# Expert tiles inside the last group iterations of a conv, attention and mixture-of-experts kernel

## The chip, the cores and the metric

The kernel runs on one core of a Trainium2 chip. The metric is the device time of one execution in microseconds (us), lower is better. The engines are TensorE (PE in the rows; PEld is its weight load), VectorE (DVE), ScalarE (ACT), GpSimd (POOL) and SyncE (SP, which only issues transfers here). Each runs its own instructions in order and waits for the others on semaphores.

## The reference

The input `x` has shape (32, 64, 16, 16). Everything is float32. Three residual blocks follow one another:

```python
x = x + conv(gn(x))        # per-channel 3x3 convolution, group norm of channel pairs
t = to_tokens(x)           # 8192 tokens of 64 channels
t = t + attn(ln(t))        # 8 heads against 32 bucket means per image, then a 64-256-64 GELU network
t = t + ffn(ln(t))         # mixture of experts
# ffn, for each token:
logits = flat @ router_w.T                  # 8 experts
gates  = the two largest softmax values, divided by their sum
h = silu(flat @ w1[e].T) * (flat @ w3[e].T) # 682 hidden units
out = sum over the two experts of gate * (h @ w2[e].T)
```

## The kernel before

**Groups.** The 32 images are worked on in 8 groups of 4 (1024 tokens). A group passes four stages: a (group norm, convolution, turn to tokens, first layer norm), b (bucket means and attention), c (second norm and GELU network), d (third norm, router, places of rows in the experts' lists). `pipeline` runs 12 iterations; in iteration i group i is in stage a, i-1 in b, i-2 in c, i-3 in d, and e=i-4 finishes on GpSimd. Each engine has its own hand-written order of the steps within an iteration, all in a function `iteration`.

**Routing.** In stage d VectorE picks two experts per token (`first_pick`, `second_pick`), TensorE counts places (`places`), VectorE turns them into row numbers (`row_places`). ScalarE copies the normed tokens into rows (`copy_rows`), and GpSimd writes them to a table in memory with 16 indirect DMAs per group (`scatter`, L497), five in the group's iteration and eleven in the next. Each expert has a region of that table.

**After the last group** TensorE counts the rows of each expert, and VectorE works out for 71 tiles of 256 rows which expert and which first row each has (`tile_expert`, `tile_row`). SyncE and ScalarE write a pad of 256 rows behind each region. SyncE then loads the weights of the tiles (four buffers) and, after all scatters have landed, their rows (eight buffers).

**A tile** t is: `turn_rows` (TensorE, two transposes), `store_xs` (ScalarE copy), three times `up(t, q)` (four matmuls of 64 rows, L757, into an h1 and an h3 bank), silu of h1 (ScalarE, L943), product with h3 (VectorE, `gated`, L1266), then `down` (six matmuls, L768), `store_results`, `turn_results`, `gate_out` (three VectorE steps, L1271 to L1277), and on GpSimd two indirect DMAs of the result rows (L519). TensorE does `up` of tile t, then `turn_rows(t+1)`, `turn_results(t-2)`, `down(t-1)`. Three h1 banks, three h3 banks and two result banks hold the tiles; all eight banks of PSUM are in use, which the group stages used before.

**The end.** When all results have landed, both result rows of a token are read back, summed with the residual and stored.

**Steps of the group stages that the text speaks of.** On GpSimd `token_rstd` (L452), `rstd2` (L458), `rstd3` (L463) raise variances to the power -1/2, `token_sum` and `unit_sum` (L468, L474) and `residual` (L481) add residuals. On VectorE `centre_scores` takes the maximum of a block of scores and subtracts it (L1096, L1098), on ScalarE `exponentials` (L848) and `store_prob` (L855) follow, on TensorE `scores` (L616), `turn_prob` (L628) and `attend` (L642). `turn_wtok` (L682) turns the third norm's tokens for the router and needs `normalise3` (L1146), which needs `rstd3`.

Of the kernel before, what the change touches and what calls it, by code (L numbers as in the profile page):

```python
# [26 lines left out]
ROW_SLOTS = 3  # L27
# [7 lines left out]
RES_SLOTS = 4  # L35
EPS = 1e-5
# [9 lines left out]
              v_heads=2 * HEADS, region=NE * NJ, scan_keep=NE * (NJ + 1), k_rows=T // MT, tile_no=1, tile_at=1,  # L46
              pad=2 * ROW, q_one=1, k_one=1)
SMALLS = dict(bias2=1, g1=1, b1=1, g2=1, b2=1, fc1_bias0=2, proj=C + M + 2 * C, fc1=DFF, fc2=2 * C, fc2_bias=C,
              router=NE)
# [14 lines left out]
def hybrid_block(nc, x, consts, smalls, weights, out):  # L64
    with ExitStack() as ctx:
# [31 lines left out]
        k_rows = const_of("k_rows")  # L97
        tile_no = const_of("tile_no")
# [64 lines left out]
        ssub = sb("ssub", [P, 2, 2 * HEADS, M])  # L163
        prob = sb("prob", [P, 2, 4, P])
# [44 lines left out]
        tile_expert = sb("tile_expert", [P, 1], U32)  # L209
        tile_row = sb("tile_row", [P, 1], U32)  # L210
# [28 lines left out]
        k_ps = bk34[0:C + 1, 0, 0:P]  # L239
        v_ps = bk34[:, 1, 0:256].rearrange("p (b c) -> p b c", b=GB)  # L240
        fc1_ps = [bk7, bk6]
        y_ps = bk7.rearrange("p (j c) -> p j c", j=NJ)
        l_ps = bk67[:, :, 0:NJ // 2 * NE].rearrange("p a (q e) -> p a q e", e=NE)
        pos_ps = bk7[:, 64:64 + NE * NJ].rearrange("p (e j) -> p e j", e=NE)
# [3 lines left out]
        xt_ps = h1_ps[0][:, 0:MT]  # L248
        yt_banks = [bk0, bk7]
# [77 lines left out]
        pos_counted = sem("pos_counted")  # L327
        sums_kept = sem("sums_kept")
# [3 lines left out]
        counted = sem("counted")  # L332
# [31 lines left out]
        def _(sp):  # L364
# [8 lines left out]
            for a in range(2, NG):  # L373
                sp.wait_ge(xn_ready, 2 * (a - 1))
                sp.wait_ge(xres_ready, 2 * (a - 1))
                load_x(a)

            sp.wait_ge(pads_ready, 1)
            write_pad(sp, NE * REG)
            for e in range(NE // 2):  # L380
                write_pad(sp, sp.value_load(pad_row[0:1, e:e + 1], min_val=0, max_val=NE * REG - MT))

            def load_weights(t):
                wait(sp, down_done, t - W_SLOTS + 1)
                expert = sp.value_load(tile_expert[t:t + 1, 0:1], min_val=0, max_val=NE - 1)
# [3 lines left out]
            def load_rows(t):  # L389
                wait(sp, y_scattered[t % X_SLOTS], 32 * (t // X_SLOTS))  # L390
                row = sp.value_load(tile_row[t:t + 1, 0:1], min_val=0, max_val=NE * REG)
# [3 lines left out]
            sp.wait_ge(sched_ready, 1)  # L395
            for t in range(W_SLOTS - 1):
                load_weights(t)
            sp.wait_ge(pads_written, 16 * (NE + 1))
            for b in range(ROW_SLOTS):
                sp.wait_ge(scattered[b], 2 * NJ * 16 * ((NG - b + ROW_SLOTS - 1) // ROW_SLOTS))  # L400
            for t in range(X_SLOTS - 2):
                load_rows(t)
            for t in range(W_SLOTS - 1, NT):
                load_weights(t)
                if t + X_SLOTS - 1 - W_SLOTS < NT:
                    load_rows(t + X_SLOTS - 1 - W_SLOTS)
# [10 lines left out]
        def _(pool):  # L417
# [8 lines left out]
            g.memset(picked[:, :, 0:1], 0.0)  # L426
            pool.wait_ge(consts_loaded, 16)
# [73 lines left out]
            def iteration(a=None, b=None, c=None, d=None, e=None):  # L501
                run(a, group_rstd)
                run(c, residual)
                run(c, rstd2)
                run(e, scatter, 5, 11)
                run(a, token_rstd)
                run(d, row_destinations)
                run(d, scatter, 0, 5)
                run(c, rstd3)
                run(a, token_sum)  # L510
                run(a, unit_sum)

            pipeline(iteration)

            for t in range(NT):
                pool.wait_ge(yout_ready, t + 1)
                pool.sem_inc(waited, 1)
                for h in range(2):
# [4 lines left out]
                        .then_inc(y_scattered[t % X_SLOTS], 16)  # L523

        @block.tensor
        def _(pe):
# [49 lines left out]
            def queries(b):  # L576
                wait(pe, probt_ready, 4 * b)
                for h in range(2):
                    last = mm(bk34[0:C + 1, h, :], q_aug[:, :], n1t[:, h * 512:(h + 1) * 512], start=True, stop=True)
                last.then_inc(q_ready, 1)  # L580
# [15 lines left out]
            def keys(b):  # L596
                pe.wait_ge(pooledt_ready, b + 1)
                pe.wait_ge(qt_ready, b + 1)
                mm(k_ps, k_aug[:, :], pooled_t[:, :], start=True, stop=True).then_inc(k_ready, 1)

            def values(b):
                pe.wait_ge(rep_ready, b + 1)
                pe.wait_ge(qt_ready, b + 1)
                for m in range(GB):
                    last = mm(bk34[:, 1, m * C:(m + 2) * C].rearrange("p (r c) -> p r c", r=2),
# [4 lines left out]
            def scores(b, p):  # L610
                if p == 0:
                    pe.wait_ge(kblk_ready, b + 1)
                wait(pe, ssub_ready, 4 * b + p - 1)
                for bp in range(2):
                    j, m = 2 * p + bp, 2 * (p // 2) + bp
                    last = mm(bk12[:, p % 2, bp * 256:(bp + 1) * 256], qt[:, j * P:(j + 1) * P],  # L616
                              kblk[:, m, :, :].rearrange("c h m -> c (h m)"), start=True, stop=True)
                last.then_inc(s_ready, 1)

            def turn_prob(b, p):  # L620
                pe.wait_ge(prob_ready, 4 * b + p + 1)
                if p == 0:
                    pe.wait_ge(kblk_ready, b + 1)
                if p == 1:
                    pe.wait_ge(vblk_ready, b + 1)
                wait(pe, probt_ready, 4 * b + p - 1)
                for a in range(4):
                    last = turn(bk34[:, p % 2, a * P:(a + 1) * P], prob[:, p % 2, a, :], ident)  # L628
                last.then_inc(probt_turned, 1)

            def attend(b, p):
                pe.wait_ge(probt_ready, 4 * b + p + 1)
                if p == 0:
                    pe.wait_ge(vblk_ready, b + 1)
                    wait(pe, att_read, 2 * b)
                if p == 2:
# [11 lines left out]
            def turn_n2(c):  # L648
                pe.wait_ge(n2_ready, c + 1)
                wait(pe, lsub_ready, c)  # L650
                for q in range(NJ // 2):
                    last = turn(bk6[:, q * P:(q + 1) * P], n2[:, 2 * q:2 * q + 2, :].rearrange("p a c -> p (a c)"), ident)
                last.then_inc(n2_turned, 1)

            def fc1(c, a):
                if a == 0:
                    pe.wait_ge(n2t_ready, c + 1)
                    wait(pe, pos_ready, c)
                for par in range(2):
                    if a == 1:  # L660
                        pe.wait_ge(hid_ready, 4 * c + par + 1)
                    at = slice(par * C, (par + 1) * C)
                    mm(fc1_ps[par], fc1_s[at, a * P:(a + 1) * P], n2t[at, :], start=True, stop=True)\
                        .then_inc(fc1_ready, 1)

            def fc2(c):
                pe.wait_ge(hid_ready, 4 * c + 4)
                for q in range(NJ // 2):
                    for par in range(2):
                        j = 2 * q + par  # L670
                        n = min(2, NJ - j)
                        for a in range(2):
                            last = mm(y_ps[:, j:j + n, :], hid[:, a, par, q * P:(q + 1) * P],  # L673
# [4 lines left out]
            def turn_wtok(c):  # L678
                pe.wait_ge(wtok_ready, c + 1)
                pe.wait_ge(hid_ready, 4 * c + 4)  # L680
                for q in range(NJ // 2):
                    last = turn(bk6[:, q * P:(q + 1) * P], wtok[:, 2 * q:2 * q + 2, :].rearrange("p a c -> p (a c)"), ident)  # L682
                last.then_inc(wt_turned, 1)

            def router(d):
                pe.wait_ge(wt_ready, d + 1)
                pe.wait_ge(t2_ready, d + 1)
                for q in range(NJ // 2):
                    for par in range(2):
                        at = slice(par * C, (par + 1) * C)  # L690
# [712 lines left out]
```

## Time and profile before

| | us |
|---|---|
| runs shown | 805.01, 802.60, 799.39 (median 802.6) |
| the profiled execution | 802.19 |
| its span, first to last instruction | 800.4 |
| TensorE busy | 650.6 (81%) |
| VectorE, ScalarE, GpSimd busy | 463.2, 353.7, 371.8 |

Busy time is a sum over stages that have different limits; a busy TensorE is not one at its peak, and its granted clock, 0.851 in the mean, has the two levels 0.5 (1.2 GHz) and 1 (2.4 GHz). What bounds a stage is read from that stage.

### The profile page before, as it was taken

The numbers are of one execution on the slowest core, as the hardware profiler recorded it, in microseconds if no ns is written. First come the engines' busy times: TensorE is split into PE (matmuls) and PEld (weight loads), VectorE is DVE, ScalarE is ACT, GpSimd is POOL, SyncE is SP. The second block draws the span as 40 slices with busy tenths as digits, with TensorE's granted clock in tenths as the row PEclk, the third lists the DMA queues.
The fourth block names the chain that finished last, engine by engine and source line by source line (L and its number), as shares of the span: only waits on it lengthen the run. The fifth ranks groups of instructions, "written<-read, shape, count | busy, mean of one in ns | idle before, by whom it ended". The sixth has DMA issues, their size and how long they took to land.

```text
span 800.4 us, 13968 instructions
## 1 busy us (share of the span) xinstructions
PE 650.6 (81%) x4632; PEld 487.2 (61%) x4632; DVE 463.2 (58%) x1094; ACT 353.7 (44%) x693; POOL 371.8 (46%) x377
## 2 busy tenths in 40 slices
PE   2597989797979797866206999999999999999960
PEld 2475858585857576664104777677777777777740
DVE  2356677686868676643502566655555665555545
ACT  1143646373727273533203555455555445555520
POOL 2204241767676768727670343334444333444440
PEclk9667868797978788575656999999999999999995
DMA  2000000010101010101173455555556455554608
GB/s 85 0 14 1 14 1 14 19 49 17 51 18 38 18 38 17 51 5 53 50 182 86 148 161 160 165 161 162 179 161 167 152 168 168 179 156 150 191 8 314
DMA packets 46615, 75.47 MB, mean 94 GB/s; under 512 B 7488, under 2 KB 30048, under 8 KB 46544
## 3 DMA queue, kind: packets, MB, share of 16 engines
q1 hardware_dynamic: 34512, 57.12, 24.5%
q0 software_dynamic: 8640, 12.74, 4.8%
q10 hardware_dynamic: 3392, 4.73, 1.8%
q8 instruction: 37, 0.61, 0.3%
q14 instruction: 34, 0.28, 0.1%
HBM read 58.54 MB, written 16.47 MB: 94 GB/s over the span
## 4 chain that ended last, share of the span: by engine, by line
PE 49%; POOL 23%; issue 17%; DVE 6%; DMA 3%; ACT 1%; POOLq 0%; SPq 0%; ACTq 0%; DVEq 0%
PE bk L757 25%; POOL expert_rows L497 15%; PE bk L768 12%; PE bk L745 3%; POOL rr L452 3%; PE bk L775 2%; POOL r L463 1%; PE bk L554 1%; POOL r L458 1%; POOL x2t L481 1%; DMA out<-hid 1%; DMA srow<-expert_results 1%; PE bk L642 1%; POOL grstd L441 1%; PE bk L616 1%
## 5 line engine op out<-in xcount | busy, mean ns | idle before, releaser
L1266 DVE TENSOR_TENSOR units<-bk,silu 128x512 f32<-128x512 f32 x213 | 147.3, 692 | 165.7 <-ACT silu L943 165.7
L519 POOL DMA_INDIRECT expert_results<-yout,xin x142 | 139.5, 983 | 218.3 <-DVE yout L1277 191.5
L757 PE MATMUL bk<-xs,wbuf 64*128 64x256 f32 x1704 | 205.5, 388 | 1.1 <-ACT xs L930 1.1
L757 PEld LDWEIGHTS bk<-xs,wbuf 64*128 64x128 f32 x1704 | 160.8, 189 | 44.4 <-issue 26.6
L943 ACT ACTIVATE silu<-bk 128x512 f32<-128x512 f32 x213 | 127.2, 597 | 87.2 <-PE bk L757 87.2
L497 POOL DMA_INDIRECT expert_rows<-srow,pos x128 | 132.4, 1034 | 44.2 <-issue 37.9
L768 PE MATMUL bk<-units,wbuf 128*64 128x256 f32 x852 | 107.6, 388 | 0.0
L768 PEld LDWEIGHTS bk<-units,wbuf 128*64 128x64 f32 x852 | 54.8, 136 | 32.4 <-issue 11.7
L935 ACT ACTIVATE ysb<-bk 128x256 f32<-128x256 f32 x71 | 27.2, 383 | 84.3 <-PE bk L768 84.3
L452 POOL TENSOR_TENSOR rr<-vare,c_mhalf 128x16 f32<-128x16 f32 x8 | 23.4, 2923 | 74.6 <-DVE vare L1046 74.6
L745 PE MATMUL bk<-const,xin 128*128 128x128 f32 x142 | 31.3, 302 | 29.2 <-DMA xin<-expert_rows 29.2
L745 PEld LDWEIGHTS bk<-const,xin 128*128 128x128 f32 x142 | 14.3, 141 | 52.5 <-issue 52.5
L930 ACT ACTIVATE xs<-bk 128x256 f32<-128x256 f32 x71 | 26.8, 378 | 34.7 <-PE bk L745 34.7
L642 PEld LDWEIGHTS bk<-vblk,prob_t 128*128 128x128 f32 x256 | 35.4, 205 | 6.9 <-ACT prob_t L855 5.0
L642 PE MATMUL bk<-vblk,prob_t 128*128 128x144 f32 x256 | 38.5, 308 | 0.2 <-ACT prob_t L855 0.2
L616 PE MATMUL bk<-kblk,qt 65*128 65x256 f32 x128 | 37.8, 435 | 0.0
L554 PE MATMUL bk<-const,hsum 128*128 128x128 f32 x192 | 35.0, 333 | 0.0
L848 ACT ACTIVATE prob<-ssub 128x512 f32<-128x512 f32 x32 | 19.4, 626 | 34.1 <-DVE ssub L1098 34.0
L1096 DVE TENSOR_REDUCE smax<-bk 128x16 f32<-128x512 f32 x32 | 21.8, 681 | 21.3 <-PE bk L616 21.2
L673 PEld LDWEIGHTS bk<-small,hid 128*128 128x128 f32 x256 | 31.2, 200 | 2.4 <-ACT hid L871 2.4
L616 PEld LDWEIGHTS bk<-kblk,qt 65*128 65x128 f32 x128 | 26.7, 226 | 9.2 <-DVE ssub L1098 5.3
L554 PEld LDWEIGHTS bk<-const,hsum 128*128 128x128 f32 x192 | 32.1, 246 | 0.0
(184 smaller groups left out, 963.2 us busy)
## 6 DMA issues: line engine op xcount, KB each, us to landing
wbuf<-in_weights SPq DMA_DIRECT2D x71, 576.0 KB, 4.1
xin<-expert_rows SPq DMA_DIRECT2D x71, 130.0 KB, 2.4
expert_results<-yout,xin POOLq DMA_INDIRECT x142, 2.8
xg<-in_x SPq DMA_DIRECT2D x8, 256.0 KB, 2.8
expert_rows<-srow,pos POOLq DMA_INDIRECT x128, 2.4
srow<-expert_results SPq DMA_DIRECT2D x8, 256.0 KB, 5.1
srow<-expert_results ACTq DMA_DIRECT2D x8, 256.0 KB, 5.9
out<-hid ACTq DMA_DIRECT2D x8, 256.0 KB, 5.2
```

The lines of the kernel that those rows point to most:

```text
L452: g.tensor_tensor(rr[:, :, :].rearrange("p a j -> p (a j)"), vare1[:, :, :].rearrange("p a j -> p (a j)"), c_mhalf[:, :], ALU.pow).then_in ...
L497: g.indirect_dma_start(rows[0:NE * REG, :], bass.IndirectOffsetOnAxis(ap=pos[:, d, k, j:j + 1], axis=0), srow[:, d % ROW_SLOTS, k, j, :], ...
L519: g.indirect_dma_start(results[:, :], bass.IndirectOffsetOnAxis(ap=xin[:, t % X_SLOTS, h, ROW - 1:ROW].bitcast(U32), axis=0), yout[:, t % ...
L554: last = mm(o, hsum[:, s, h0 + dy:h0 + dy + 8, :], ident, start=False, stop=dy == 2)
L616: last = mm(bk12[:, p % 2, bp * 256:(bp + 1) * 256], qt[:, j * P:(j + 1) * P], kblk[:, m, :, :].rearrange("c h m -> c (h m)"), start=True, ...
L642: last = mm(bk5[:, at:at + 2 * (C + HEADS)].rearrange("p (r c) -> p r c", r=2), prob_t[:, p % 2, 2 * bp + ch, :], vblk[:, m, ch, :].unsque ...
L673: last = mm(y_ps[:, j:j + n, :], hid[:, a, par, q * P:(q + 1) * P], fc2_s[:, a, :].unsqueeze(1).broadcast_to([P, n, C]), start=a == 0, sto ...
L745: last = turn(xt_ps[:, h * P:(h + 1) * P], xin[:, t % X_SLOTS, h, 0:2 * C], ident)
L757: last = mm(bank[:, ch * MT:(ch + 1) * MT], wbuf[part, t % W_SLOTS, at:at + P], xs[part, t % 2, :], start=True, stop=True)
L768: last = mm(yt_banks[t % 2][ch * C:(ch + 1) * C, 0:MT], wbuf[:, t % W_SLOTS, at:at + C], units[:, t % 2, q, ch * MT:(ch + 1) * MT], start= ...
L943: f(silu[:, q, :], h1_ps[q], ACT.Silu).then_inc(silu_ready, 1)
L1266: tt(units[:, t % 2, q, :], h3_ps[q], silu[:, q, :], ALU.mult).then_inc(unit_ready, 1)
```

## The change

The pipeline stays as it is for iterations 0 to 4 (`ramp`). From iteration 5 (`MIX`) to 10 the iterations are mixed (`mix`): in each, 16 slots between group steps hold beats, and a beat is a third of an expert tile, one `up(t, q)` with what hangs on it. `slot_beats` gives 27 beats (nine tiles) to iteration 5, none in its slots 0 to 4, and 24 (eight tiles) to the others: one in each of slots 0 to 7, two in each of slots 8 to 15. The score and attention steps stand between slots 9 and 10 with no beats. The 49 mixed tiles are followed by a tail of 22 in the old order.

The tiles of a round come from `schedule(d)`, which runs on VectorE behind each group from d = 1 and picks tiles whose 256 rows are full by then; the last round, for the tail, takes the rest. A round's first `load_rows` waits for the scatters of all groups up to its own. All 16 scatters of a group now run in the group's own iteration, in iterations 5 to 10 four by four behind `token_rstd` and between slots 10 to 13.

PSUM is divided anew in the mixed part: three banks are a ring for h1 and h3 (two per beat), one bank (`bk7`) holds the turned rows and the results of a tile, one bank (`shared`) in turn holds scores, n2, y and wtok, one (`turned`) queries, values and turned probabilities. Probabilities before the turn get four buffers where they had two; row buffers go from three to two. The router multiplies both halves of its input at once. The expert counts come from `places` of each group. All nine pads are written by SyncE.

```diff
+MIX = 5
+FIRST_ROUND = 1
+ROUND_TILES = [0, 9, 8, 8, 8, 8, 8]
+MIXED = sum(ROUND_TILES)
+SLOTS_A, SLOTS_S = 10, 6
-ROW_SLOTS = 3
+ROW_SLOTS = 2
+def slot_beats(i):
+    if i == MIX:
+        return [0, 0, 0, 0, 0, 2, 2, 2, 2, 2, 3, 3, 3, 3, 3, 2]
+    return [1, 1, 1, 1, 1, 1, 1, 1, 2, 2, 2, 2, 2, 2, 2, 2]
...
+        ring = [bk12[:, 1, :], bk34[:, 1, :], bk6]
+        def ring_banks(k):
+            return ring[2 * k % 3], ring[(2 * k + 1) % 3]
...
@@ SyncE
             def load_rows(t):
+                r = ROUND_OF[t]
+                s = t - ROUND_AT[r]
+                if s == 0:
+                    for b in range(ROW_SLOTS):
+                        sp.wait_ge(scattered[b], 2 * NJ * 16 * ((r - b) // ROW_SLOTS + 1))
...
+            def beat(t, q):
+                if q == 0:
+                    load_tile(t + W_SLOTS - 1)
@@ GpSimd
+            def beat(t, q):
+                if q == 2 and t > 0:
+                    scatter_results(t - 1)
+            def mixed_iteration(i, a=None, b=None, c=None, d=None):
+                run(c, residual)
+                beats(i, 0, beat)
+                beats(i, 1, beat)
+                run(c, rstd2)
+                run(d, rstd3)
+                beats(i, 2, beat)
+                run(a, group_rstd)
+                for k in range(3, SLOTS_A):
+                    beats(i, k, beat)
+                run(d, row_destinations)
+                run(a, token_rstd)
+                run(d, scatter, 0, 4)
+                beats(i, 10, beat)
+                run(d, scatter, 4, 4)
+                beats(i, 11, beat)
+                run(d, scatter, 8, 4)
+                run(a, token_sum)
+                run(a, unit_sum)
+                beats(i, 12, beat)
+                run(d, scatter, 12, 4)
+                beats(i, 13, beat)
...
@@ TensorE
+            def ring_free(k):
+                for earlier, first in ((k - 2, False), (k - 1, True)):
...
+                        elif first:
+                            pe.wait_ge(silu_ready, NU * x + y + 1)
+                        else:
+                            pe.wait_ge(unit_ready, NU * x + y + 1)
...
+            def turn_rows(t):
+                pe.wait_ge(xin_loaded[t % X_SLOTS], 16 * (t // X_SLOTS + 1))
+                if t < MIXED:
+                    wait(pe, yout_ready, t - 2)
...
+            def beat(t, q):
...
+                up(t, q)
+                if q == 0 and t + 1 < MIXED:
+                    turn_rows(t + 1)
+                if q == 1 and t > 0:
+                    down(t - 1)
+                if q == 2 and t > 0:
+                    turn_results(t - 1)
...
+                beats(i, 9, beat)
+                run(b, scores, 0)
+                run(a, convolution, 0)
+                run(b, scores, 1)
+                run(a, convolution, 1)
+                run(b, scores, 2)
+                run(d, places)
+                run(b, scores, 3)
+                run(b, turn_prob, 0)
+                run(b, turn_prob, 1)
+                run(c, fc1, 0)
+                run(b, attend, 0)
+                run(b, attend, 1)
+                run(b, turn_prob, 2)
+                run(c, fc1, 1)
+                run(b, turn_prob, 3)
+                run(b, attend, 2)
+                run(b, attend, 3)
+                beats(i, 10, beat)
+                run(c, fc2)
...
@@ ScalarE, slots 0, 1 and 7 to 10
+                run(b, store_n1t, 1)
+                beats(i, 0, beat)
+                run(c, squares2)
+                run(d, squares3)
+                beats(i, 1, beat)
...
+                run(a, add_x)
+                run(b, key_blocks)
+                beats(i, 7, beat)
+                run(d, copy_rows)
+                run(c, store_n2t)
+                beats(i, 8, beat)
+                beats(i, 9, beat)
+                run(d, router_exp)
+                run(b, exponentials, 0)
+                run(b, exponentials, 1)
+                run(a, store_tokens)
+                run(b, exponentials, 2)
+                run(b, exponentials, 3)
+                run(b, store_prob, 0)
+                run(b, store_prob, 1)
+                run(a, squares1)
+                run(c, gelus, 0)
...
@@ VectorE, score part
+                run(b, centre_scores, 0)
+                run(d, first_pick)
+                run(b, centre_scores, 1)
+                run(d, second_pick)
+                run(b, centre_scores, 2)
+                run(a, centre1)
+                run(d, row_places)
+                run(b, centre_scores, 3)
+                run(a, variance1)
+                run(b, attended, 0)
+                run(d, schedule)
+                run(a, normalise1)
+                run(b, attended, 1)
+                beats(i, 10, beat)
```

## Rows read from the trace of the kernel before

**Rows 1.** windows: us, busy of PE, PEld, DVE, ACT, POOL, then PEclk, DMA share, GB/s
```profile
182.04:222.99 40.95, 34.85 (x226) 27.75 (x224) 30.74 (x80) 22.02 (x43) 29.63 (x28) 0.83 0.10 33
401.00:427.40 26.40, 0.66 (x2) 0.29 (x2) 0.00 (x0) 0.40 (x2) 14.68 (x16) 0.50 0.62 146
433.60:761.40 327.80, 327.80 (x2718) 233.22 (x2718) 193.51 (x406) 166.12 (x339) 129.70 (x132) 1.00 0.54 162
```

**Rows 2.** timeline of GpSimd in iterations 4 and 5; start, duration, engine, line, output and input
```profile
176.13 2.93 POOL L452 TENSOR_TENSOR rr<-vare,c_mhalf 128x16 f32<-128x16 f32 x1 [3.15 <-DVE vare L1046]
...
187.02 2.13 POOL L463 TENSOR_TENSOR r<-vare,c_mhalf 128x8 f32<-128x8 f32 x1
189.13 1.27 POOL L468 TENSOR_TENSOR u_tok<-tok,small 128x512 f32<-128x512 f32 x1
190.48 1.59 POOL L474 TENSOR_TENSOR u_tok<-u_tok,u 128x512 f32<-128x512 f32 x1
...
196.20 1.26 POOL L481 TENSOR_TENSOR x2t<-u_tok,att 128x512 f32<-128x512 f32 x1
197.42 1.67 POOL L458 TENSOR_TENSOR r<-vare,c_mhalf 128x8 f32<-128x8 f32 x1
```

**Rows 3.** timeline of TensorE at the start of iteration 5; idle time before in brackets
```profile
182.04 2.21 PE L642 MATMUL bk<-vblk,prob_t 128*128 128x144 f32 x16
...
192.35 0.59 PE L544 MATMUL bk<-chvar,const 128*128 128x2 f32 x2 [4.41 <-DVE chvar L1016]
192.80 1.09 PE L682 MATMUL bk<-const,wtok 128*128 128x128 f32 x4
```

**Rows 4.** timeline of all engines over one expert tile
```profile
520.21 2.86 PE L757 MATMUL bk<-xs,wbuf 64*128 64x256 f32 x24
...
521.38 0.60 ACT L943 ACTIVATE silu<-bk 128x512 f32<-128x512 f32 x1 [0.66 <-PE bk L757]
...
522.00 0.69 DVE L1266 TENSOR_TENSOR units<-bk,silu 128x512 f32<-128x512 f32 x1 [1.56 <-ACT silu L943]
...
523.59 1.52 PE L768 MATMUL bk<-units,wbuf 128*64 128x256 f32 x12
...
524.34 0.28 DVE L1271 COPY ysum<-bk 128x128 f32<-128x128 f32 x1
...
524.98 0.29 DVE L1277 TENSOR_TENSOR yout<-ysum,xin 128x128 f32<-128x128 f32 x1
...
525.03 2.86 PE L757 MATMUL bk<-xs,wbuf 64*128 64x256 f32 x24
```

**Rows 5.** timeline from the last scatters to the first tile
```profile
419.57 0.96 POOL L497 DMA_INDIRECT expert_rows<-srow,pos  x1 [0.30 <-issue]
420.83 0.96 POOL L497 DMA_INDIRECT expert_rows<-srow,pos  x1 [0.30 <-issue]
...
426.28 0.66 PE L745 MATMUL bk<-const,xin 128*128 128x128 f32 x2 [29.21 <-DMA xin<-expert_rows]
```

**Rows 6.** timeline of VectorE in the routing and score steps
```profile
201.90 0.22 DVE L1161 SCALAR_TENSOR_TENSOR peq<-lsub,const 128x64 f32<-128x64 f32 x1
...
207.74 0.69 DVE L1096 TENSOR_REDUCE smax<-bk 128x16 f32<-128x512 f32 x1 [0.96 <-PE bk L616]
...
214.35 0.69 DVE L1098 TENSOR_TENSOR ssub<-bk,smax 128x512 f32<-128x512 f32 x1
```

**Rows 7.** groups by line and shape: count, busy us, mean ns, idle before and its releaser
```profile
L519 POOL DMA_INDIRECT expert_results<-yout,xin x142 | 139.5, 983 | 218.3 <-DVE yout L1277 191.5 <-issue 26.8
...
L848 ACT ACTIVATE prob<-ssub 128x512 f32<-128x512 f32 x32 | 19.4, 626 | 34.1 <-DVE ssub L1098 34.0
...
L848 ACT ACT_TABLE_LOAD x7 | 9.0, 1283 | 0.1
...
L886 ACT ACTIVATE srow<-wtok 128x1024 f32<-128x1024 f32 x16 | 16.1, 1064 | 0.0
```

**Rows 8.** windows, one stretch of iteration 6; columns as in rows 1
```profile
231.00:241.20 10.20, 7.91 (x43) 4.40 (x43) 6.02 (x19) 2.60 (x4) 7.16 (x9) 0.50 0.01 2
```

More of the change, by code:

```diff
@@ L499, in scatter, with scatter_results @@
                         srow[:, d % ROW_SLOTS, k, j, :], None).then_inc(scattered[d % ROW_SLOTS], 16)
[L501 to L515, printed above, removed]
+            def scatter_results(t):
                 pool.wait_ge(yout_ready, t + 1)
@@ L574, in rotate, with queries @@
                 last.then_inc(rot_ready, 1)
[L576 to L580, printed above, removed]
+            def queries(b, h):
+                if h == 0:
+                    wait(pe, probt_ready, 4 * b)
+                elif mixed(b + 1):
+                    pe.wait_ge(qt_ready, 2 * b + 1)
+                mm(q_bank(b, h)[0:C + 1, :], q_aug[:, :], n1t[:, h * 512:(h + 1) * 512], start=True, stop=True)\
+                    .then_inc(q_ready, 1)
             def bucket_sums(b):
@@ L697, in places @@
                 pe.wait_ge(passed_ready, d + 1)
-                mm(pos_ps, before, picked[:, :, 1:NJ + 1], start=True, stop=False)
-                mm(pos_ps, ones, passed[:, :, 0:NJ], start=False, stop=True).then_inc(pos_counted, 1)
-            def iteration(a=None, b=None, c=None, d=None, e=None):
+                if mixed(d + 3):
+                    if d + 2 < NG:
+                        pe.wait_ge(kblk_ready, d + 3)
+                    pe.wait_ge(att_read, 2 * min(d + 2, NG))
+                bank = place_bank(d)
@@ L732, in iteration @@
                 run(a, turn_n1, 0)
-            pipeline(iteration)
-            pe.wait_ge(sums_kept, NG)
-            pe.wait_ge(pos_ready, NG)
-            mm(bk7[:, 0:NE], ones, picked[:, :, 0], start=True, stop=True).then_inc(counted, 1)
-            pe.wait_ge(sched_ready, 1)
-            def turn_rows(t):
-                pe.wait_ge(xin_loaded[t % X_SLOTS], 16 * (t // X_SLOTS + 1))
-                wait(pe, silu_ready, NU * (t - 1) + 1)
-                for h in range(2):
-                    last = turn(xt_ps[:, h * P:(h + 1) * P], xin[:, t % X_SLOTS, h, 0:2 * C], ident)
-                last.then_inc(xt_turned, 1)
@@ L780, in _ @@
+            ramp(iteration)
+            mix(mixed_iteration)
+            turn_rows(MIXED)
+            for t in range(MIXED, NT):
                 for q in range(NU):
@@ L1205, in iteration, with beat @@
+            def beat(t, q):
+                gated(t, q)
+                if q == 2 and t > 0:
+                    gate_out(t - 1)
+            def iteration(i, a=None, b=None, c=None, d=None, e=None):
                 run(a, channel_statistics)
```

674 lines of the change are left out of this document (467 added, 207 removed).

## The prediction, made before the result

> **What bounds the kernel now.** I read the windows by stage first, then the timelines of GpSimd and TensorE, then the groups. The run has four parts: eight group iterations, their drain, a gap, and 71 expert tiles. A full group iteration takes 40.95 us and TensorE is busy for 34.85 of it, part of that at the lower clock; the gap costs 26.4 us with TensorE all but idle; in the tiles TensorE is busy 327.80 of 327.80 us at full clock [rows 1]. So the tiles are bound by TensorE, and nothing in them waits. A group iteration is bound by GpSimd's queue: sixteen scatters, 1.26 us from one to the next [rows 5], are 20.2 us, and with the power instructions and sums [rows 2] the queue has some 35 us of work in 41.
>
> The change wants to put tiles into TensorE's idle time. There is less of it than the page suggests. At full clock the group steps of an iteration are about 31 us of TensorE (34.85 less half of the 7.91 that it is busy in a stretch like the one at 1.2 GHz [rows 1, 8]); eight tiles are 8 x 4.82 = 38.6 (520.21 to 525.03, [rows 4]); together 69.5 against 40.95 + 38.6 = 79.5 now. Only if the mixed iteration comes under 79.5 does it gain.
>
> **Up to the first tile.** TensorE starts iteration 5 at 182.0 [rows 3], in both kernels. In the new GpSimd order iteration 4 issues all sixteen scatters of group 1 behind the token power (176.13 to 179.06): 0.85 wait for the iota and 16 x 1.265 end them at 200.2; two sums (1.27, 1.59) at 203.1; then residual 1.26, second and third power 1.67 and 2.13 [rows 2]: 208.2. normalise3 and the transposes of wtok stand behind that; now they start at 192.8 [rows 3], then at about 210. Rows turned and copied, the first `up` starts at 213. That is 31 us of iteration 5 for group steps that took about 20.
>
> **A tile in the mixed part** has one result bank and three ring banks, so each `up` waits for the silu of the beat before it. The prices are read from [rows 4]: the silu ends 1.77 after its `up` starts (521.38 + 0.60 - 520.21), the product 0.71 later, gate_out's three steps 0.93 later still (524.34 to 525.27). turn_rows of the next tile waits for that gate_out: 3.46 after the last `up` of the tile before. Then turn 0.3, `up` 0.93, `down` 1.45, and the next last `up` starts at 6.15. So a bare mixed tile takes 6.15 where it now takes 4.82; group steps of TensorE can fill the difference only in the slots that have any.
>
> **A full mixed iteration (6 and 7)**, followed along its queues:
> - Slots 0 to 9 (four tiles and the first group half): TensorE's work is 19.3 + about 11. Where it stands still: 1.4 for the squares, which wait on ScalarE ahead of a silu until VectorE has done channel statistics and two centrings; 2.5 in pair_variances, whose VectorE step is behind two variances; 2.3 for a silu behind key_blocks, copy_rows (2 x 1.06, [rows 7]) and n2t; 3 in several short ones. Sum 39.4.
> - The score part, one score bank and no tiles. VectorE's order is gate_out of the last tile (ends 2.25 after TensorE starts the part), four centre_scores, first_pick, second_pick, centre1, row_places. Now the same steps run from 201.90 to 215.04 with one centre_scores fewer (1.40), normalise2 (0.6), vblk (0.7) and a wait (0.96) more [rows 6]: 12.3 to 12.8. Then exp 0.63 [rows 7], prob copy, turn, copy, squares (0.6 each) and a reduction with two small steps, 0.9: the variance for token_rstd is ready 19.4 after the start. TensorE is through at 25.
> - GpSimd from there: power 2.93, 16 scatters 20.2, results of two tiles 4 x 1.285 = 5.1 (0.98 each plus issue, [rows 7]), two sums 2.9, and 3.7 waiting, since the results of tile 3 are gated out only 36 after the part's start while GpSimd reaches them earlier. Sum 34.8.
> - The next round's first tile may hold rows of this group: SyncE holds its row load until all sixteen scatters landed, and TensorE turns those rows right behind `up(7,0)`, in order. From the end of the last scatter to the turn it is 4.5 now (421.79 to 426.28, [rows 5]). TensorE gets to this turn 23 after the score part's end by bare tiles, some 11 before the rows are there. Behind it stand turn 0.3, two `up`, `down` and a turn: 3.9.
> 39.4 + 19.4 + 34.8 + 4.5 + 3.9 = 102.
>
> ScalarE switches tables up to three times in such an iteration (exp, gelu, silu), where the group steps alone need two. A load takes 1.28 and no idle time stands behind it: the idle time before the exponentials is all VectorE's [rows 7]. Two of the three loads lie under VectorE's list, the gelu's is in the 25 above. The Trainium skill (ScalarE: Activation LUTs, What ACT_TABLE_LOAD costs) adds a drain of about 1.4 to each load; by that the sum would be some 7 us higher. The row decides against it.
>
> The new `schedule`, 17 small VectorE steps, is about 4.3 by the row of the smallest steps (0.2 each and more, [rows 6]); it has attended's wait beside it in iterations 5 to 8 and costs nothing there, and about 4 in iterations 9 and 10, where the next products are queued behind it. SyncE's loads of the other seven tiles are issued two tiles ahead: nothing, or a row load of about 2 if SyncE is late. SyncE writes the pads, all nine now, with the load for the tail's first tile, three tiles ahead: the same late scatters hide them.
>
> **The others.** Iteration 5 has nine tiles in slots 5 to 15: 23 for slots 5 to 9, 25 for scores, 5.7 x 6.15 + 3.6 (fc2) less 0.6 for the rest, 2.6 at the row wait: 89, ending at 302. Iteration 8 has no a-stage: 34 to the scores, row_places at 12.4, then scatters, results (waiting until tile 3's at 34.9) and row load to 58.5: 93. Iteration 9 has c and d only: 32 + 46 = 78. Iteration 10: 28 + 38.6 = 66.5 to the first tail rows.
>
> **The tail.** From the first turned rows to the end of the span is now 374.1 us for 71 tiles [rows 5]; less 49 x 4.82 = 236.2 it is 138 for 22. The profiled run lies 1.8 over its span.
>
> **Sum:** 182 + 31 + 89 + 102 + 102 + 93 + 78 + 66.5 + 138 + 1.8 = 883. The clock: TensorE stood still for 4.41 us before 192.35 [rows 3] and likewise one iteration later, and from 231.0 to 241.2 it was granted 0.50, the lower level of 1.2 GHz [rows 8]. The waits of 4 in the score part and 11 at the rows should bring such stretches too. That costs nothing where VectorE or GpSimd ends last, and up to 4 + 3 in an iteration where the tiles do: 0 to 33 over six. I take 7, as the late scatters cover most of it. **Forecast 890**, against 802.19 of the profiled run, which is within 0.1% of the median of 802.6, so it is taken for that too.
>
> **Rivals.**
> 1. *GpSimd keeps up*: the scatters go out fast enough that rows never hold TensorE. For: its queue has some 53 us of work in 100. Against: the order puts all scatters behind token_rstd. Then iterations end by TensorE's own chain (39.4 + 25 + 28 = 92.4; 85, 70, 62 for the last): 182 + 120 + 185 + 217 + 138 + 2 = 844; were slots 0 to 9 free of stalls too (7.4 less in iterations 6 and 7, some 6 in 5 and 8), 817. Chance 0.20.
> 2. *The clock* is at its lower level wherever waits break up the beats, and the products and scatters follow: 883 + 33 = 916. For: [rows 8]. Against: TensorE has more work between waits than now. The Trainium skill (TensorE: Matmul & The Clock Gate, Loop structure matters more than you think) holds that matmuls parted by waits run cold and the loop nest decides it; by that rule this rival holds, and [rows 3, 8] agree for a wait of 4.4. Chance 0.20.
> 3. *Faster*: TensorE is the bound, tiles and group steps fill each other. Iterations then take 69.5, and 65, 47, 41 for the last three. With iteration 5 ending at 280 (210, nine tiles 43, the other group steps some 25): 280 + 139 + 153 + 138 + 2 = 712 at the very best, 797 with half of the 171 us between it and the sum; so it is faster if more than half of my waits are not there, or the six iterations average under 80 from 182 on ((802 - 1.8 - 138 - 182) / 6). I put it at 770. For: VectorE has only 30.74 + 8 x 3 = 55 of work in such an iteration [rows 1, 4]. Against: the score part alone holds VectorE for 15 us before the fourth ssub. Chance 0.08; another 0.04 that gains and losses cancel.
> 4. The forecast's case: 0.48.
>
> **Range and chances.** 815 to 930: from the first rival's low end to the second's 916 with a row load late in each iteration (6 x 2). Within 1% is what runs of this kernel can't tell from none (799.4 to 805.0). Faster 0.08, same 0.04, slower 0.88.
>
> **What would show it.** GpSimd's line of scatters directly behind rr, ending late in slot 12 or after; TensorE idle some 10 us per iteration before a turn of xin, released by the DMA of expert_rows; a wait of about 4 in each score part before turn_prob; first `up` near 213; the tail beginning near 745. I am wrong if mixed iterations come in at 80 or less, if the wait for rows is missing (then near 845), or if TensorE's clock is low for most of the mixed part.

## The result, and the profile after

The changed kernel takes 929.7 us (median of 4; 927.3 to 934.6) against 801.2 of the kernel before beside it: 1.161 times as long, 95% interval 1.158 to 1.164. The forecast was 890, range 815 to 930, "slower" at 0.88. The direction came out and most of the waits did; the size did not, by 40 us: the time lies at the upper end of the range. The profiled execution took 934.56, its span is 932.5, and all times below are from it.

The page of the changed kernel: span, TensorE's row of busy time, the granted clock in 40 slices, and the shares of the chain that ended last.
```profile
span 932.5 us, 14259 instructions
PE 709.0 (76%) x4582; PEld 487.2 (52%) x4582; DVE 476.2 (51%) x1206; ACT 365.8 (39%) x708; POOL 366.7 (39%) x378
PEclk9576977968899888977989778888978979899995
PE 44%; DVE 17%; issue 13%; POOL 12%; ACT 7%; DMA 5%; SPq 0%; POOLq 0%; ACTq 0%; DVEq 0%
```
The clock row is the first thing to see: four slices in a row at 9 come only in the tail. VectorE, behind which no tile of the kernel before waited, has 17% of the chain, and TensorE is idle for 24% of the span that was to be filled.

The timeline of TensorE at the six turns of rows that had to wait for the row load (in brackets the wait):
```profile
303.32 0.44 PE L866 MATMUL bk<-const,xin 128*128 128x128 f32 x2 [3.88 <-DMA xin<-expert_rows]
412.77 0.69 PE L866 MATMUL bk<-const,xin 128*128 128x128 f32 x2 [10.07 <-DMA xin<-expert_rows]
523.34 0.69 PE L866 MATMUL bk<-const,xin 128*128 128x128 f32 x2 [11.32 <-DMA xin<-expert_rows]
628.78 0.69 PE L866 MATMUL bk<-const,xin 128*128 128x128 f32 x2 [8.39 <-DMA xin<-expert_rows]
717.64 0.69 PE L866 MATMUL bk<-const,xin 128*128 128x128 f32 x2 [7.83 <-DMA xin<-expert_rows]
793.24 0.69 PE L866 MATMUL bk<-const,xin 128*128 128x128 f32 x2 [5.28 <-DMA xin<-expert_rows]
```
These turns mark out the iterations, so the sum can be laid against them. The prediction's terms for iterations 5 to 7 end 3.9 behind a turn, so their turns were at 302 - 3.9 = 298.1 and so on; those for 8 to 10 end at the turn itself (in iteration 8 the 58.5 runs up to the row load):

| turn of rows that ends | predicted at | measured at | interval predicted | measured |
|---|---|---|---|---|
| iteration 5 | 298.1 | 303.32 | | |
| iteration 6 | 400.1 | 412.77 | 102 | 109.45 |
| iteration 7 | 502.1 | 523.34 | 102 | 110.57 |
| iteration 8 | 599 | 628.78 | 96.9 | 105.44 |
| iteration 9 | 677 | 717.64 | 78 | 88.86 |
| iteration 10 (tail's first rows) | 743.5 | 793.24 | 66.5 | 75.60 |
| end of the span | 881.5 | 932.5 | 138 | 139.3 |

Every mixed iteration is longer than predicted; the first turn (+5.2) and the tail (+1.3) are nearly right.

Windows over iteration 6 of the changed kernel, columns as in [rows 1]:
```profile
309.20:321.10 11.90, 8.43 (x64) 5.88 (x62) 10.10 (x19) 4.45 (x9) 3.24 (x3) 0.99 0.43 128
321.10:334.80 13.70, 12.69 (x56) 6.08 (x56) 7.41 (x24) 3.18 (x7) 7.38 (x8) 0.51 0.02 5
334.80:353.00 18.20, 15.34 (x115) 10.19 (x114) 8.49 (x20) 12.42 (x31) 4.00 (x4) 1.00 0.29 88
365.50:372.30 6.80, 3.96 (x13) 2.16 (x13) 2.40 (x7) 3.92 (x6) 0.64 (x1) 0.51 0.00 0
402.70:412.80 10.10, 0.03 (x2) 0.03 (x1) 0.98 (x2) 0.60 (x1) 6.38 (x7) 0.67 0.18 52
412.80:418.70 5.90, 5.90 (x33) 3.44 (x34) 0.69 (x1) 1.55 (x4) 0.00 (x0) 0.69 0.38 121
```
The second row is the one the prediction priced too low: for 13.7 us TensorE is granted the lower level, 1.2 GHz, while it is busy for 12.69 of them (7.91 of 10.20 in [rows 8]). The work itself runs at half speed and, as experiment 2 shows, sets the end. What went before it is short: waits of 2.29 and 1.21 us, at 319.39 and 322.11. The last two rows are the wait for the rows and the 5.9 us behind it, where turn, two `up`, `down` and a turn were put at 3.9.

### The profile page after: what moved, and what is told of

Same layout as the page of the kernel before. It is cut to its first block, busy times and chain, and to the rows that moved or that the text cites. A ratio compares the mean times of both kernels' runs of the same rounds, so it can differ in the third digit from the quotient of the medians.

```text
span 932.5 us, 14259 instructions
## 1 busy us (share of the span) xinstructions
PE 709.0 (76%) x4582; PEld 487.2 (52%) x4582; DVE 476.2 (51%) x1206; ACT 365.8 (39%) x708; POOL 366.7 (39%) x378
## 4 chain that ended last, share of the span: by engine, by line
PE 44%; DVE 17%; issue 13%; POOL 12%; ACT 7%; DMA 5%; SPq 0%; POOLq 0%; ACTq 0%; DVEq 0%
PE bk L883 17%; PE bk L899 9%; POOL expert_rows L576 7%; ACT silu L1142 3%; PE bk L773 2%; DVE units L1543 2%; PE bk L821 2%; PE bk L809 2%; PE bk L866 2%; POOL expert_results L584 2%; PE bk L696 2%; DMA expert_rows<-srow,pos 2%; DMA xin<-expert_rows 1%; DMA srow<-expert_results 1%; DVE ssub L1388 1%
## 5 line engine op out<-in xcount | busy, mean ns | idle before, releaser
L883 PE MATMUL bk<-xs,wbuf 64*128 64x256 f32 x1704 | 251.5, 425 | 37.0 <-ACT silu L1142 33.7
L883 PEld LDWEIGHTS bk<-xs,wbuf 64*128 64x128 f32 x1704 | 166.8, 202 | 103.4 <-issue 72.0
L576 POOL DMA_INDIRECT expert_rows<-srow,pos x128 | 127.5, 996 | 55.4 <-issue 38.8
L899 PE MATMUL bk<-units,wbuf 128*64 128x256 f32 x852 | 119.6, 421 | 0.0
L899 PEld LDWEIGHTS bk<-units,wbuf 128*64 128x64 f32 x852 | 59.5, 148 | 48.5 <-issue 30.7
L773 PE MATMUL bk<-vblk,prob_t 128*128 128x144 f32 x256 | 40.6, 315 | 1.1 <-ACT prob_t L1089 1.1
L757 PE MATMUL bk<-const,prob 128*128 128x128 f32 x128 | 22.5, 308 | 16.1 <-ACT prob_t L1089 12.4
L669 PE MATMUL bk<-const,hsum 128*128 128x128 f32 x192 | 33.0, 319 | 0.0
L739 PEld LDWEIGHTS bk<-kblk,qt 65*128 65x128 f32 x128 | 23.8, 204 | 15.8 <-DVE ssub L1388 12.7
L906 PE MATMUL bk<-const,ysb 128*128 128x128 f32 x142 | 30.6, 298 | 1.0 <-ACT ysb L1136 1.0
```

The lines of the kernel that those rows point to most:

```text
L576: g.indirect_dma_start(rows[0:NE * REG, :], bass.IndirectOffsetOnAxis(ap=pos[:, d, k, j:j + 1], axis=0), srow[:, d % ROW_SLOTS, k, j, :], ...
L669: last = mm(o, hsum[:, s, h0 + dy:h0 + dy + 8, :], ident, start=False, stop=dy == 2)
L739: last = mm(score_bank(b, p)[:, bp * 256:(bp + 1) * 256], qt[:, j * P:(j + 1) * P], kblk[:, m, :, :].rearrange("c h m -> c (h m)"), start= ...
L773: last = mm(bk5[:, at:at + 2 * (C + HEADS)].rearrange("p (r c) -> p r c", r=2), prob_t[:, p % 2, 2 * bp + ch, :], vblk[:, m, ch, :].unsque ...
L883: last = mm(bank[:, ch * MT:(ch + 1) * MT], wbuf[part, t % W_SLOTS, at:at + P], xs[part, t % 2, :], start=True, stop=True)
L899: last = mm(y_bank(t)[ch * C:(ch + 1) * C, 0:MT], wbuf[:, t % W_SLOTS, at:at + C], units[:, t % 2, q, ch * MT:(ch + 1) * MT], start=q == 0 ...
```

## Experiments

Kernels are the changed one with the edits named; ratios are to the kernel before, on the same chip. Fill matmuls are matmuls whose results nothing reads.

**1. Scatters early.** If rows hold TensorE because twelve scatters stand behind token_rstd and the sums, issuing them right behind the first four must remove the wait.
```
-                run(d, scatter, 4, 4)
+                run(d, scatter, 4, 12)
...
-                run(d, scatter, 8, 4)
...
-                run(d, scatter, 12, 4)
```


> One change to the new kernel: on GpSimd the twelve scatters that stood behind slots 10, 11 and 12 follow the first four at once. Theory R (TensorE waits for rows because GpSimd issues a group's last scatters late): in iteration 6 the power ends at 374.6, 16 x 1.27 later is 394.9, the rows are turned 4.5 later at 399.4, and TensorE asks for them at 402.7. The waits of 3.9, 10.1, 11.3, 8.4, 7.8 and 5.3 us before the turns of xin are gone, 47 us, and the half clock behind them, some 2 each: 870 to 885. Rival (another wait takes its place, the tiles' results now late or the next group step): 915 or more.

Measured 880.0 us, ratio 1.097 (1.093 to 1.101): 50 us back. GpSimd's timeline in iteration 6, first of the changed kernel, then of this one:
```profile
371.66 2.94 POOL L531 TENSOR_TENSOR rr<-vare,c_mhalf 128x16 f32<-128x16 f32 x1 [13.30 <-DVE vare L1336]
...
390.78 1.00 POOL L584 DMA_INDIRECT expert_results<-yout,xin  x1 [5.29 <-DVE yout L1554]
...
407.36 0.96 POOL L576 DMA_INDIRECT expert_rows<-srow,pos  x1 [0.31 <-issue]
```
```profile
365.74 2.93 POOL L531 TENSOR_TENSOR rr<-vare,c_mhalf 128x16 f32<-128x16 f32 x1 [13.31 <-DVE vare L1334]
...
388.61 0.96 POOL L576 DMA_INDIRECT expert_rows<-srow,pos  x1 [0.30 <-issue]
389.87 1.00 POOL L584 DMA_INDIRECT expert_results<-yout,xin  x1 [0.31 <-issue]
```
From the power to the last scatter's start it is 35.7 in the changed kernel and 22.9 here. In between stood 5.29 of waiting for a result, four result scatters and two sums; results and sums now come behind, and nothing waits. Of the row waits only the tail's is left (5.03 at 740.13), which was expected to go too. The low clock in the slots stays: slots 0 to 9 of iteration 6 still take 43.7 (303.43 to 347.15), so the row waits are not what brings it. Iteration 6 shrinks by 11.6, from 109.5 (309.18 to 418.69) to 97.9 (303.43 to 401.31): the wait of 10.07, and most of the 2.0 of low clock behind it.

**2. Fill matmuls in the short waits.** If the clock costs the rest, feeding TensorE in the waits of slots 0 to 9 and of the score part must give time back though it adds work.
```
                 run(b, rotate)
+                if b is not None:
+                    pe.wait_ge(t2_ready, i - 2)
+                    fill(5, shared)
                 beats(i, 2, beat)
+                if a is not None:
+                    fill(3, shared)
                 run(a, pair_variances)
...
                 run(b, turn_prob, 0)
+                if a is not None:
+                    pe.wait_ge(tok_ready, a + 1)
+                if b is not None:
+                    fill(8 if a is not None else 4)
...
```
In iterations 8 to 10 there are some more of them between the scores and ahead of places.

> One change to the new kernel: TensorE fills its other waits with matmuls whose results nobody reads (ident by the constants, 128x256), 5 after rotate and 3 before pair_variances in slots 1 and 2, and 8 between turn_prob 0 and 1; in iteration 8 also 5 and 4 in place of the convolution and 4 between turn_prob 0 and 1, in 9 and 10 twelve before places. It costs TensorE time only where a wait stood. Theory C (the 40 us that my sum lacks are the lower clock behind short waits): the stretches at 0.5 in slots 2 to 5 and in the score part shrink, iterations 6 to 8 are 6 to 10 us shorter, 9 and 10 some 4: 890 to 910. Rival (the clock is not the cause, the sum lacks other waits): 925 to 940, the fills cost what they take.

Measured 905.4 us, ratio 1.129 (1.125 to 1.133): 24 us back. Windows over slots 0 to 9 of iteration 6 and over the rest up to the turn, in the changed kernel and in this one:
```profile
309.20:353.10 43.90, 36.57 (x234) 22.25 (x233) 26.00 (x61) 20.14 (x46) 14.62 (x15) 0.84 0.24 73
353.10:412.80 59.70, 40.87 (x277) 29.26 (x275) 28.81 (x83) 21.48 (x36) 29.87 (x28) 0.89 0.19 60
```
```profile
303.50:341.60 38.10, 34.15 (x250) 22.64 (x249) 25.82 (x61) 20.02 (x46) 14.39 (x15) 1.00 0.28 84
341.60:400.80 59.20, 44.06 (x293) 32.72 (x291) 28.86 (x83) 21.41 (x36) 29.80 (x28) 0.91 0.19 61
```
The slots take 38.1 at clock 1.00 with 16 instructions more, 43.9 at 0.84 without them: 5.8 us of clock. The prediction's 39.4, made for full clock, holds. The score part and the scatters behind it take 59.2 and 59.7, where 58.7 was predicted (19.4 + 34.8 + 4.5): there VectorE and GpSimd end last and TensorE's clock buys nothing.

Iteration 7 did not gain like this. The stretch at the lower level went from the middle of the slots and came back at their end, behind a wait of 1.62 at 440.38; the first of the slow `up`s, which takes 1.13 at full clock:
```profile
442.54 2.08 PE L883 MATMUL bk<-xs,wbuf 64*128 64x256 f32 x8
```
The slots take 41.1 there (408.06 to 449.12), and from the turn of rows before (400.76) to its own (511.05) iteration 7 is 0.3 shorter than in the changed kernel, where 6 to 10 were expected. Iteration 6 is 6.0 shorter, 8 is 8.3, 9 is 3.0 and 10 is 1.9 (their turns at 297.28, 608.21, 694.07 and 767.82).

**3. Both.**

> Both edits of the two kernels before. If R and C hold and don't overlap, the gains add up: 840 to 860. If the rows and the clock are one cause (the long wait brings all of the low clock), the result is that of the early scatters alone, 870 to 885.

Measured 858.7 us, ratio 1.072 (1.068 to 1.077): 71 us back, 50 and 24 nearly added. Its windows over the same stretches:
```profile
303.60:341.70 38.10, 34.16 (x250) 22.63 (x249) 25.82 (x61) 20.02 (x46) 14.39 (x15) 1.00 0.27 84
341.70:395.60 53.90, 48.26 (x324) 35.28 (x323) 29.54 (x84) 22.97 (x40) 29.74 (x28) 0.97 0.25 79
```
An iteration is 92.0 (303.61 to 395.61), the first rival's 92.4. So without the row waits and most of the low clock the change still loses 57 us: 92 is over the 79.5 that eight tiles and an iteration take apart.

**4. Order at the start.** Iteration 4 keeps the third power ahead of the eleven scatters, which would let wtok (the third norm's tokens, turned for the router), and with it the first tile, go earlier if that power held the start up.
```
-                if last:
-                    run(d, scatter, 5, 11)
-                else:
-                    run(c, rstd3)
+                run(c, rstd3)
...
+                if i == MIX:
+                    run(d - 1, scatter, 5, 11)
```


> On the new kernel: iteration 4 keeps the old order on GpSimd (five scatters, then the third power), and the other eleven scatters of group 1 follow in iteration 5 behind the three powers. If my reading of the start is right (sixteen scatters and four other steps in a row, the first tile can't start before group 1 has landed): the transposes of wtok come 18 us earlier, near 193, but the first tile's rows are turned at 214 to 218, no earlier than now (212.5), and the total is the same within 5 us. Rival (the late third power alone holds the first tile): the first up comes 10 us or more earlier and the total falls by as much.

One execution, 937.2 us. TensorE's timeline, of the changed kernel and of this one:
```profile
211.62 1.11 PE L833 MATMUL bk<-const,wtok 128*128 128x128 f32 x4 [8.59 <-DVE wtok L1436]
...
214.67 1.65 PE L883 MATMUL bk<-xs,wbuf 64*128 64x256 f32 x6 [1.50 <-ACT xs L1131]
```
```profile
198.25 1.12 PE L833 MATMUL bk<-const,wtok 128*128 128x128 f32 x4
...
219.49 0.66 PE L866 MATMUL bk<-const,xin 128*128 128x128 f32 x2 [20.12 <-DMA xin<-expert_rows]
```
The turn of wtok comes 13 earlier, and the first rows, now behind later scatters, come at 219.5 instead of 212.5, later than the 214 to 218 expected. What it gives it takes: the first tile is bound by group 1's scatters whichever goes first. The total is 2.6 over the profiled execution of the changed kernel; a single run shows no more than that nothing was won.

**5. Tiles in iterations 9 and 10 alone.** With MIX = 9 no iteration that holds all of a, b, c and d is mixed; scatters early. If a mixed drain fills time that TensorE idles anyway, this beats the kernel before.
```
-MIX = 5
-FIRST_ROUND = 1
-ROUND_TILES = [0, 9, 8, 8, 8, 8, 8]
+MIX = 9
+FIRST_ROUND = MIX - 4
+ROUND_TILES = [0] * FIRST_ROUND + [9] + [8] * (10 - MIX)
```


> Mixed iterations start at 9 in place of 5 (17 mixed tiles, 54 in the tail), with the early scatters. Where the old pipeline drains, TensorE has little group work and the old kernel stood still for 26 us before its first tile. Theory M (mixing loses where a group iteration is full, since each queue's order and the score part then hold the tiles, and gains only in the drain): iterations 9 and 10 take some 90 and 65 for 17 tiles: 780 to 800, at or a little under the kernel before. Rival (tiles mixed in lose anywhere, by their own 6.2 us and the late scatters): 815 or more.

Measured 806.6 us, ratio 1.006 (1.004 to 1.008). A miss: 73 us better than experiment 1, which has the same scatters, but not faster. Part of what is lost stands in the bare tiles, whose turns of rows are 6.3 apart:
```profile
428.24 0.41 PE L864 MATMUL bk<-const,xin 128*128 128x128 f32 x2 [0.44 <-DVE yout L1552]
...
432.99 1.14 PE L881 MATMUL bk<-xs,wbuf 64*128 64x256 f32 x8 [0.40 <-ACT silu L1140]
434.56 0.41 PE L864 MATMUL bk<-const,xin 128*128 128x128 f32 x2 [0.44 <-DVE yout L1552]
```

**6. The same with a fourth ring bank.** In iterations 9 and 10 the banks of steps a and b are free: one joins the ring, and turned rows go into the convolution's. The waits for a free bank are loosened to match.
```
-        ring = [bk12[:, 1, :], bk34[:, 1, :], bk6]
+        ring = [bk12[:, 1, :], bk34[:, 1, :], bk6, turned]
...
-            return bk7[:, MT:2 * MT] if t < MIXED else h1_ps[0][:, 0:MT]
+            return bk0[:, 0:MT] if t < MIXED else h1_ps[0][:, 0:MT]
```


> The kernel that mixes from iteration 9 with early scatters (806.6), with one thing more: in those two iterations no image is in the first two stages, so the bank of queries and turned probabilities joins the ring (four banks) and the turned rows go to the bank of the convolution. A beat then waits for the one two before it, not for the last silu, and turn_rows not for gate_out. Theory T (a mixed tile costs 6.15 to 6.3 us in place of 4.82 because of three ring banks and one result bank): 17 tiles x 1.3 = 22 us less: 780 to 792. Rival (the mixed tiles are held by the other queues, not by banks): 800 to 808.

Measured 792.4 us, ratio 0.987 (0.984 to 0.990): 1.3% faster than the kernel before. The same turns:
```profile
407.54 0.44 PE L859 MATMUL bk<-const,xin 128*128 128x128 f32 x2
...
412.91 0.44 PE L859 MATMUL bk<-const,xin 128*128 128x128 f32 x2
...
418.29 0.44 PE L859 MATMUL bk<-const,xin 128*128 128x128 f32 x2
```
5.4 apart and without a wait. Over 17 mixed tiles 0.95 each are 16 us; 14 came back, where 22 were expected. Most of what a bare mixed tile takes over 4.82 [rows 4] is the sharing of banks.

**7. Iteration 10 alone.** As 6, but MIX = 10 and nine tiles.

> The same with mixing in iteration 10 alone: nine mixed tiles, 62 in the tail. They run while the last group is routed and scattered, where the kernel before had TensorE idle for 26 us (401 to 427). Theory M (mixing pays where the pipeline drains): 780 to 792, about that of mixing from 9, since iteration 9 has still a full c-stage. Rival (iteration 9's own waits are the larger gain): 795 to 805.

Measured 799.7 us, ratio 0.997 (0.996 to 0.999), the rival's number. TensorE's waits show where it went:
```profile
399.13 1.11 PE L828 MATMUL bk<-const,wtok 128*128 128x128 f32 x4 [18.21 <-DVE wtok L1427]
...
428.01 0.69 PE L849 MATMUL bk<-picked,const 128*128 128x64 f32 x2 [5.17 <-DVE passed L1464]
...
467.75 0.69 PE L859 MATMUL bk<-const,xin 128*128 128x128 f32 x2 [5.87 <-DMA xin<-expert_rows]
```
Wherever mixing begins, the iteration ahead of it puts the scatters before the third power, and wtok pays once: 18.2 here, 12.0 in experiment 6. One mixed iteration covers little more than that.

**8. Scores first.** On experiment 3: the four centre_scores ahead of the routing picks on VectorE, places behind fc1.
```
                 run(b, centre_scores, 0)
-                run(d, first_pick)
                 run(b, centre_scores, 1)
-                run(d, second_pick)
                 run(b, centre_scores, 2)
                 run(a, centre1)
-                run(d, row_places)
                 run(b, centre_scores, 3)
+                run(d, first_pick)
+                run(d, second_pick)
                 run(a, variance1)
+                run(d, row_places)
```


> On the new kernel with early scatters and warm fills (858.7): VectorE does the four centre_scores first and first_pick, second_pick and row_places behind them, TensorE's places stands behind fc1. Theory S (the score part is held by VectorE's list, in which the routing steps stand between the scores): the fourth ssub comes 3 to 4 us earlier in iterations 5 to 8, the turned probabilities with it, and the parts shorten by 2 to 4 each: 845 to 853. Rival (one score bank holds it, each scores waits for the ssub before, whatever stands between): 856 to 862.

Measured 857.2 us, ratio 1.070 (1.065 to 1.075), against 858.7: nothing, as the rival had it. Yet the score part did get shorter, from 24.95 (341.68 to 366.63) to 23.4 (337.83 to 361.25). Windows over the last beats ahead of it and over most of it, of experiment 3 and of this one:
```profile
337.40:341.70 4.30, 4.21 (x33) 2.65 (x34) 1.38 (x2) 1.80 (x5) 1.94 (x2) 1.00 0.05 17
341.70:366.60 24.90, 22.25 (x128) 17.88 (x126) 17.59 (x60) 12.58 (x19) 7.07 (x6) 0.93 0.11 36
```
```profile
332.00:338.00 6.00, 5.82 (x33) 3.52 (x34) 1.42 (x3) 2.04 (x5) 1.95 (x2) 0.72 0.04 12
338.00:361.00 23.00, 19.91 (x125) 16.32 (x125) 17.61 (x58) 12.27 (x19) 8.05 (x7) 1.00 0.13 41
```
A short stretch at the lower level lay inside the score part; it now lies ahead of it, in 33 instructions that take 5.8 instead of 4.2. From the last waiting turn to the first `up` behind the part it is 29.1 in both (337.49 to 366.63, 332.18 to 361.25). Why the stretch moved, no run shows.

**9. Fill matmuls in the fastest version.** On experiment 6, in its four waits: 40 ahead of the first turn of wtok, 16 ahead of each places, 26 ahead of the tail's rows.

> The kernel with tiles in iterations 9 and 10 alone, four ring banks and early scatters (792.4 us), with fill matmuls whose results nothing reads where TensorE waits: 40 before the first turn of wtok (12.0 us of waiting), 16 before each places (5.2 and 5.4), 26 before the turned rows of the tail (8.0). Theory C (a wait leaves TensorE at 1.2 GHz for a while after it, and that is lost where TensorE ends last): behind each of the four waits about 8 to 10 us of work run at half clock in that kernel, 3 to 4 us lost each; with the fills 780 to 787. Rival (the late part is bound by the rows' arrival and by the waits' own ends, so the clock after them changes little): 790 to 794.

Measured 792.0 us, ratio 0.986 (0.984 to 0.988): the same as without, the rival's case. TensorE's timeline at the tail's first rows, of experiment 6 and of this one:
```profile
492.23 0.69 PE L859 MATMUL bk<-const,xin 128*128 128x128 f32 x2 [8.02 <-DMA xin<-expert_rows]
...
498.02 0.44 PE L859 MATMUL bk<-const,xin 128*128 128x128 f32 x2
```
```profile
490.07 11.39 PE L843 MATMUL bk<-const 128*128 128x256 f32 x52
501.30 0.38 PE L864 MATMUL bk<-const,xin 128*128 128x128 f32 x2
504.94 0.44 PE L864 MATMUL bk<-const,xin 128*128 128x128 f32 x2
```
The next turn follows 3.6 behind the rows instead of 5.8, so the fills do their work. But each takes 0.44, and 26 of them take 11.4 where the wait was 8.0; the first 40 end 5.2 after wtok is there (366.14 + 0.69, and the turn at 372.00). What the clock gives back, the surplus of fills takes: they were too many, and fewer were not tried.

## Why the prediction was right in direction and wrong in size

**Right.** TensorE is not free to fill: the iteration's chain runs through VectorE's score list and GpSimd's scatters, and in iteration 6 with fills it is 38.1 + 59.2 against a predicted 39.4 + 58.7. The row wait was named at "some 11" and is 10.07 and 11.32, and early scatters remove it. The tail for 22 tiles was 138, measured 139.3. The score part's power starts 18.6 after the part (353.06 to 371.66), predicted 19.4, and from there to the end of the last scatter (408.32) it is 36.7, predicted 34.8: that their sum fits so well is partly luck. The bare mixed tile was worked out at 6.15; from the last `up` of one to that of the next it is 6.33 in the changed kernel:
```profile
393.34 1.14 PE L883 MATMUL bk<-xs,wbuf 64*128 64x256 f32 x8
...
396.82 0.41 PE L866 MATMUL bk<-const,xin 128*128 128x128 f32 x2 [0.44 <-DVE yout L1554]
...
399.67 1.13 PE L883 MATMUL bk<-xs,wbuf 64*128 64x256 f32 x8
```
The wait on yout, the one result bank, stands where it was put.

Table loads cost no more than their row. In the changed kernel (groups of ScalarE: busy, mean ns, idle before):
```profile
L1105 ACT ACT_TABLE_LOAD x8 | 10.3, 1283 | 0.1
L1142 ACT ACT_TABLE_LOAD x7 | 9.0, 1283 | 0.1
L1126 ACT ACT_TABLE_LOAD x6 | 7.7, 1283 | 0.1
```
There are 25 of them in all, at 1283 ns, and nothing like a drain stands ahead of them. The Trainium skill (ScalarE: Activation LUTs, What ACT_TABLE_LOAD costs) has the same 1283 and a drain beside it; these rows show the first and not the second.

**Wrong: the clock term.** The step that failed is "I take 7, as the late scatters cover most of it". The runs show some 30 in the slots and behind the row waits alone. Slots 0 to 9 are not covered by the scatters of their own iteration, which are issued later; there TensorE ends last, and each of iterations 6 to 8 loses some 6: 43.9 against 38.1 with fills; 43.8 in iteration 7 (418.69 to 462.44) against 38.1 in experiment 3 (395.61 to 433.69); 41.0 (530.24 to 571.25) against 35.0 with fills (517.82 to 552.82) in iteration 8. That is about 17.5. Behind the row waits the beats run at the lower level too, here in iteration 8, where an `up` takes 1.13 and `down` 1.52 at full clock:
```profile
629.40 2.08 PE L883 MATMUL bk<-xs,wbuf 64*128 64x256 f32 x8
631.41 2.83 PE L899 MATMUL bk<-units,wbuf 128*64 128x256 f32 x12
```
From the turn of rows to the turn of results it is 5.6, 5.7, 6.6, 6.8 and 6.8 behind the five waits, and 3.95 in experiment 3 (391.39 to 395.34): some 12 more. So the term is about 30, an estimate from these rows. Experiment 2 fills no row wait; of the 24 that it gave back, 3.0 and 1.9 lie in iterations 9 and 10, which the 30 leaves out. With them the clock comes to some 34, at the prediction's upper bound of 33 or past it; that bound is itself less than six times the 4 + 3 that it names. The Trainium skill (TensorE: Matmul & The Clock Gate, Loop structure matters more than you think) says that the loop nest decides whether matmuls stay warm and that a long DMA wait between them makes them cold; the `up` of 2.08 behind the row wait agrees. Here waits of only 1.2 to 2.3 us between beats, none of them for a DMA, also went ahead of such a stretch. The second rival, at 0.20 and 916, was the nearest to the result, and its mechanism came out in the slots and behind the row waits.

**What else the sum lacked.** Of the 51.6 between 883, the sum ahead of the clock term, and the profiled 934.56, the clock is some 34. The terms for iterations 8 and 9 leave out the 3.9 behind the row wait, which 5, 6 and 7 have: 7.8. The first row wait ended 5.2 late, of which 1.7 were there at the first `up` (214.67 for 213) and 2.9 went with the fills of experiment 2, so are clock too (from the first scores of iteration 5 to the turn, 238.80 to 303.32 and 235.62 to 297.28). The other 4 or so are smaller differences, such as iteration 7 from the scores on (60.9 against 58.7), and were not run down one by one.

**The third rival (faster)** fell on its price. With row waits and most of the low clock removed an iteration is still 92.0 and not 69.5. Of the 22.5 between them bank sharing explains up to 8 x 0.95 = 7.6, if it costs here what it did in experiment 6. The score part, 25 us without a tile in it, is the other large block; that it holds the rest is not shown, since experiment 8 took 1.5 off it and lost as much ahead of it.

## What to carry to other kernels

Before filling one stage's idle time with another stage's work, price the filled stage from its own chain and compare it with the two apart; here 92 against 79.5 decides, and mixing paid only where the host stage is thin (iterations 9 and 10, 0.987). Work that another engine is waiting for, like these scatters, goes first in its queue, ahead of all that only feeds the next iteration. A clock term is to be priced by asking in each stretch which engine ends last; where that is TensorE, take the upper bound.

## What the runs showed of the hardware

The lower clock level is granted to a busy TensorE too: 13.7 us at 0.51 with 12.69 us of work. Unread matmuls in waits of a few us brought the slots of iteration 6 to 1.00, and over the whole run they were worth 24 us of 930. A stretch at the lower level that goes away in one place can come back in another (experiment 2 in iteration 7, experiment 8).
